# A low-rank adapter and a mixture of experts on one core: logits turned by transposes, h turned inside down for the last tiles, smaller first loads

## The reference

```python
# x [4, 512, 512]; adapter of a batch row a = itok[b]
base = einsum('bsi,oi->bso', x, W_base)
h    = einsum('bsi,ji->bsj', x, Wt)
z    = einsum('bsj,brj->bsr', h, A[a])            # rank 16
l    = einsum('bsr,bor->bso', z, B_w[a])
y    = base + einsum('bso,po->bsp', l, Wp) * scaling[a]
logits = y @ gate_w.T                             # 16 experts
w, e = top_k(softmax(logits), 2);  w = w / sum(w)
g, u = y @ w_gate[e].T, y @ w_up[e].T             # 512 -> 352
out  = x + sum_k w_k * (silu(g) * u) @ w_down[e].T
```

## Time and profile before

| | |
|---|---|
| median of 3 runs | 377.56 us (377.18 to 378.63) |
| the profiled execution | 377.08 us, its span 375.1 us |
| busy share of the span | PE 95%, PEld 84%, DVE 52%, ACT 48%, POOL 34% |
| the chain that ended last | PE 82%, DVE 8%, DMA 4% |
| moved by DMA | 74.26 MB, mean 198 GB/s |

### The profile page before, as it was taken

One profiled execution on the slowest core, in us unless ns is written; L12 is line 12 of the kernel. 1 busy time (PEld: TensorE's weight loads), 2 busy tenths in 40 slices (PEclk: granted clock), 3 DMA queues, 4 the chain that ended last, 5 costly groups with the idle time before them and its releaser, 6 DMA issues.

```text
span 375.1 us, 7604 instructions
## 1 busy us (share of the span) xinstructions
PE 356.9 (95%) x2069; PEld 316.7 (84%) x2069; DVE 195.1 (52%) x269; ACT 178.3 (48%) x242; POOL 128.9 (34%) x85
## 2 busy tenths in 40 slices
PE   8999999998899999999999999999999999999970
PEld 4677787787789999999999999999999999999940
DVE  0485599793264627272654826548262655654210
ACT  1487621521455463645547455474555456644120
POOL 0000000023513524554454645546355455132311
PEclk9999999999899999999999999999999999999986
DMA  7994753736877675949487794857948476822230
GB/s 249 407 476 149 288 197 108 276 109 232 294 259 222 169 249 89 314 92 315 85 244 215 225 310 82 260 187 215 311 93 262 110 223 189 260 32 30 32 55 7
DMA packets 29632, 74.26 MB, mean 198 GB/s; under 512 B 3776, under 2 KB 3904, under 8 KB 29504
## 3 DMA queue, kind: packets, MB, share of 16 engines
q1 hardware_dynamic: 20624, 54.79, 41.7%
q0 software_dynamic: 8960, 18.89, 23.2%
HBM read 61.08 MB, written 19.92 MB: 216 GB/s over the span
## 4 chain that ended last, share of the span: by engine, by line
PE 82%; DVE 8%; DMA 4%; issue 2%; SPq 2%; ACT 1%; POOL 0%; ACTq 0%; DVEq 0%; POOLq 0%
PE bank L626 40%; PE bank L643 22%; PE bank L559 5%; PE bank L604 3%; PE bank L397 2%; PE bank L498 2%; PE bank L500 2%; PE bank L499 2%; DMA wb_sb<-wb 2%; SPq L342 2%; DMA xg<-y_rows,gidx 1%; DVE oh_m L1001 1%; PE bank L425 1%; PE bank L480 1%; DMA y_rows<-y_st 1%
## 5 line engine op out<-in xcount | busy, mean ns | idle before, releaser
L1111 POOL DMA_INDIRECT out<-ys,sidx x40 | 70.2, 1756 | 141.2 <-ACT ys L772 72.7
L1094 POOL DMA_INDIRECT xg<-y_rows,gidx x40 | 58.2, 1455 | 97.9 <-issue 88.0
L336 DVE TENSOR_TENSOR w_lo<-w_raw,w_hi (+2 forms) x32 | 76.1, 2379 | 21.4 <-ACT w_hi L334 19.2
L626 PE MATMUL bank<-w_hi,xt_hi 128*128 x320 | 80.5, 333 | 0.0
L626 PE MATMUL bank<-w_hi,xt_lo 128*128 x320 | 77.2, 322 | 0.0
L626 PE MATMUL bank<-w_lo,xt_hi 128*128 x320 | 77.1, 322 | 0.0
L334 ACT ACTIVATE w_hi<-w_raw (+2 forms) x32 | 64.8, 2024 | 6.3 <-issue 4.5
L763 ACT ACTIVATE sg<-bank 128x352 f32<-128x352 f32 x40 | 18.6, 465 | 80.7 <-PE bank L626 79.8
L626 PEld LDWEIGHTS bank<-w_hi,xt_lo 128*128 128x128 f32 x320 | 55.8, 188 | 0.0
L626 PEld LDWEIGHTS bank<-w_lo,xt_hi 128*128 128x128 f32 x320 | 55.7, 188 | 0.0
L626 PEld LDWEIGHTS bank<-w_hi,xt_hi 128*128 128x128 f32 x320 | 54.1, 189 | 0.1
(11 more groups left out here) (168 smaller groups left out, 376.7 us busy)
## 6 DMA issues: line engine op xcount, KB each, us to landing
w_raw<-wall SPq DMA_DIRECT2D x16, 1408.0 KB
w_raw<-wall SPq DMA_DIRECT2D x16, 768.0 KB
x_st<-xt SPq DMA_DIRECT2D x8, 512.0 KB, 12.9
y_rows<-y_st SPq DMA_DIRECT2D x16, 256.0 KB, 2.3
wt_sb<-wt SPq DMA_DIRECT2D x2, 512.0 KB, 5.5
wpt_sb<-wpt SPq DMA_DIRECT2D x2, 512.0 KB, 7.7
wb_sb<-wb SPq DMA_DIRECT2D x2, 512.0 KB, 7.2
wbt_sb<-wbt SPq DMA_DIRECT2D x2, 512.0 KB, 8.6
```

The costliest lines, as they stand in the source:

```text
L336: e.tensor_tensor(w_lo[:, bass.ds(dst, n)], raw, hi, ALU.subtract).then_inc(own, 1)
L626: mm = e.matmul(bank[2 + 2 * s + t % 2][:, 0:INTER], a, w[:, bass.ds(at + (k * GU + s * INTER), INTER)], start=k == 0 and a is hi and w is ...
L1094: e.indirect_dma_start(out=xg[t % NXG][:], out_offset=None, in_=y_dram, in_offset=bass.IndirectOffsetOnAxis(ap=gidx[:, t:t + 1], axis=0)). ...
L1111: e.indirect_dma_start(out=out, out_offset=bass.IndirectOffsetOnAxis(ap=sidx[:, t:t + 1], axis=0), in_=ys[t % NYS][:], in_offset=None, bou ...
```

## The change

1. **First loads.** A and B come as 64 columns each; B is repeated to 128 columns by a copy on VectorE (`bw_s`). The gate rows and the scaling lie in `cst`; a copy on VectorE spreads the gate rows (`gt_s`), and `gate_rows` writes 64 columns a part. `wt` is loaded and used in four pieces, `cst` comes ahead of `wb`, `adp` behind it.
2. **Logits.** `logits_turn` transposes the 32 rows of a chunk; VectorE sums the halves of all chunks in one reduction.
3. **Places** in TensorE's program are pairs of chunk and k: ranks two k later, table products and need_turn later, x_turn(0) inside chunk 15. On VectorE the last steps of `oh_q` come ahead of w_lo's halves for tile 0.
4. **Tiles from 32 on.** h_turn(t) stands inside down(t-1), ahead of its last k; ACT and VectorE write `ht` of tile t in iteration t, and VectorE splits gu ahead of `y_low`.
5. **The end.** SP, not POOL, waits for the last scatters.

```diff
-C_TURN, C_RANKS, C_WORDS, C_LOAD, C_SPLIT, C_TABLES, C_NEED = 3, 5, 7, 7, 10, 11, 12
+C_WORDS, C_LOAD, C_SPLIT = 7, 7, 10
+AT_TURN, AT_RANKS, AT_TABLES, AT_NEED, AT_X = (3, 1), (5, 2), (12, 1), (12, 3), (CH - 1, 2)
...
@@ SP: loads
-            for s in range(3):
-                load(small_sb[:, s], small[:, s], d_small[s])
-                big, src, done = ((wt_sb, wt, d_wt), (wpt_sb, wpt, d_wpt), (wb_sb, wb, d_wb))[s]
-                for i, half in enumerate(halves):
-                    load(big[:, half], src[:, half], done[i])
-                if s == 1:
-                    load(scl_sb[:], scl, d_scl)
-                    load(adp_sb[:], adp, d_adp)
-                    load(cs[:], cst, d_cst)
+            load(at_s[:], at, d_small[0])
+            for k in range(KH):
+                load(wt_sb[:, k], wt[:, k], d_wt[k])
+            load(bw_in[:], bw, d_small[1])
+            for i, half in enumerate(halves):
+                load(wpt_sb[:, half], wpt[:, half], d_wpt[i])
+            load(cs[:], cst, d_cst)
+            load(wb_sb[:, halves[0]], wb[:, halves[0]], d_wb[0])
+            load(wb_sb[:, halves[1]], wb[:, halves[1]], d_wb[1])
+            load(adp_sb[:], adp, d_adp)
...
@@ SP: end
+            count = tile_count(e)
+            lasts = [e.snap(((count + (NYS - 1 - i)) // NYS) * 16) for i in range(NYS)]
+            for i in range(NYS):
+                e.wait_ge(d_s[i], lasts[i])
+            e.sem_inc(p_turn, 1)
...
@@ TensorE: logits_turn
-                    mm = e.matmul(bank[5][:, c * NEXP:(c + 1) * NEXP], lt_sb[b % 2][:, r * P:(r + 1) * P],
-                                  cs[0:G2, C_RNK:C_RNK + NEXP], start=True, stop=True)
+                    mm = e.transpose(bank[5][:, c * G2:(c + 1) * G2], lt_sb[b % 2][:, r * P:(r + 1) * P], ident[0:G2, 0:G2])
...
@@ TensorE: chunks 3 to 15
-                y_base(c, range(1))
-                if c == C_TURN:
-                    logits_turn(3)
-                if c == C_RANKS:
-                    ranks()
-                y_base(c, range(1, 2))
-                if c == C_TABLES:
-                    e.wait_ge(v_ohm, 1)
-                    slot_tables(bank[4], 0, 2)
-                if c == C_NEED:
-                    need_turn()
-                y_base(c, range(2, KH))
+                for k in range(KH):
+                    if (c, k) == AT_TURN:
+                        logits_turn(3)
+                    if (c, k) == AT_RANKS:
+                        ranks()
+                    if (c, k) == AT_TABLES:
+                        e.wait_ge(v_ohm, 1)
+                        slot_tables(bank[4], 0, 2)
+                    if (c, k) == AT_NEED:
+                        need_turn()
+                    if (c, k) == AT_X:
+                        count = tile_count(e)
+                        words = {0: tile_word(e, 0)}
+                        x_turn(e, count, 0)
+                    y_base(c, range(k, k + 1))
                 y_rank(c)
...
-                if c == CH - 2:
-                    count = tile_count(e)
-                    words = {0: tile_word(e, 0)}
-                    x_turn(e, count, 0)
...
@@ TensorE: down, and the tiles
                     for k in range(KI):
+                        if t + 1 >= NFULL and t + 1 < NTILE and k == KI - 1:
+                            h_turn(t + 1)
...
-                    if t >= 3:
+                    if 3 <= t <= NFULL:
                         h_turn(t - 1)
...
@@ ACT: the tiles
-                    if t >= 3:
+                    if 3 <= t <= NFULL:
                         h_evac(t - 1)
...
                     if t < NTILE:
                         silu(t)
+                    if NFULL <= t < NTILE:
+                        h_evac(t)
                     if t + 1 < NTILE:
                         split_weights(e, count, t + 1, word, "dn", a_dn)
...
@@ VectorE: start
+            e.wait_ge(d_small[1], 16)
+            e.tensor_copy(bw_s[:].rearrange("p k (i r) -> p k i r", i=P // RR),
+                          bw_in[:].unsqueeze(2).to_broadcast([P, KH, P // RR, RR])).then_inc(v_bw, 1)
             e.wait_ge(d_cst, 16)
+            gt_in = cs[:, C_GT:C_GT + KH * NEXP].rearrange("p (k n) -> p k n", n=NEXP)
+            e.tensor_copy(gt_s[:], gt_in.unsqueeze(2).to_broadcast([P, KH, NBATCH, NEXP])).then_inc(v_gt, 1)
             e.wait_ge(d_adp, 16)
...
@@ VectorE: routing
-            lg = bank[5][:, 0:CH * NEXP].rearrange("p (c n) -> p c n", n=NEXP)
+            lg = sh2[:]
+            step(e.tensor_reduce(lg, bank[5][:].rearrange("p (c h n) -> p c n h", h=2, n=NEXP), AX_X, ALU.add))
...
@@ VectorE: the tiles
-                    if t >= 3:
+                    if 3 <= t <= NFULL:
                         h_low(t - 1)
-                    if t == 1:
+                    if t == 1 or NFULL <= t < NTILE - 1:
                         split_weights(e, count, t + 1, word, "gu", v_gu)
...
-                    if 2 <= t < NTILE - 1:
+                    if 2 <= t < NFULL:
                         split_weights(e, count, t + 1, word, "gu", v_gu)
                     if t < NTILE:
                         product(t)
+                    if NFULL <= t < NTILE:
+                        h_low(t)
                     if t + 1 < NTILE:
                         split_weights(e, count, t + 1, word, "dn", v_dn)
...
@@ POOL: end
-            lasts = [e.snap(((count + (NYS - 1 - i)) // NYS) * 16) for i in range(NYS)]
-            for i in range(NYS):
-                e.wait_ge(d_s[i], lasts[i])
-            e.sem_inc(p_turn, 1)
```

More of the change, by code:

```diff
@@ L79, with build @@
 SKIP = 4096
-C_ID, C_IQ, C_TOK, C_ADP, C_AT, C_BEF, C_TOP, C_RNK, C_SEL, CW = (
-    0, P, P + TQ, *(P + TQ + CH + i for i in range(5)), P + TQ + CH + 4 + RANK, 2 * P + TQ + CH + 4 + RANK)
+C_ID, C_IQ, C_TOK, C_ADP, C_AT, C_BEF, C_TOP, C_RNK, C_SEL, C_SCL, C_GT, CW = (
+    0, P, P + TQ, *(P + TQ + CH + i for i in range(5)), *(P + TQ + CH + 4 + RANK + i for i in (0, P, P + 1, P + 1 + KH * NEXP)))
 R_TRI, R_ONE, R_REV, R_THR, R_CUM, R_TH3, R_IM, RW = 0, P, 2 * P, 2 * P + 16, 2 * P + 32, 2 * P + 288, 2 * P + 293, 3 * P + 293
-def build(nc, cst, rcst, small, adp, scl, wt, wpt, wb, wbt, xt, x, wall, out):
+def build(nc, cst, rcst, at, bw, adp, wt, wpt, wb, wbt, xt, x, wall, out):
     with ExitStack() as ctx:
@@ L128, in build @@
         r_lo0 = region(o_lo, SLOT)
-        small_sb = r_lo0("small_sb", [P, 3, KH, P], F32)
+        at_s, bw_in = [r_lo0(n, [P, KH, RR], F32) for n in ("at_s", "bw_in")]
+        bw_s = r_lo0("bw_s", [P, KH, P], F32)
+        gt_s = r_lo0("gt_s", [P, KH, NBATCH, NEXP], F32)
         wb_sb = r_lo0("wb_sb", [P, KH, H], F32)
@@ L174, in build @@
         adp_sb = r_b("adp_sb", [P, NBATCH], I32)
-        scl_sb = r_b("scl_sb", [P, 1], F32)
         r_y = region(o_b, KH * H * 4)
@@ L219, in build @@
         y_dram = nc.dram_tensor("y_rows", [NTOK, H], F32, kind="Internal").ap()
-        d_cst, d_rc, d_adp, d_scl = [sem("d_" + n) for n in ("cst", "rc", "adp", "scl")]
-        d_small = [sem("d_" + n) for n in ("at", "bw", "gt")]
-        d_wt, d_wpt, d_wb, d_wbt = [[sem(f"d_{n}{i}") for i in range(2)] for n in ("wt", "wpt", "wb", "wbt")]
+        d_cst, d_rc, d_adp = [sem("d_" + n) for n in ("cst", "rc", "adp")]
+        v_bw, v_gt = sem("v_bw"), sem("v_gt")
+        d_small = [sem("d_" + n) for n in ("at", "bw")]
+        d_wt = [sem(f"d_wt{i}") for i in range(KH)]
+        d_wpt, d_wb, d_wbt = [[sem(f"d_{n}{i}") for i in range(2)] for n in ("wpt", "wb", "wbt")]
         d_x = [[sem(f"d_x{b}_{i}") for i in range(2)] for b in range(NBATCH)]
@@ L398, in k_sum, with low_rank @@
                 return mm
[L400 to L405, removed]
+            def low_rank(dst, a, big, landed):
+                for k in range(KH):
+                    if k * len(landed) % KH == 0:
+                        e.wait_ge(landed[k * len(landed) // KH], 16)
+                    mm = k_sum(dst, [(a[:, k], big[:, k])], first=k == 0, last=k == KH - 1)
                 return mm
@@ L1178 @@
     gt = chunks(get["L0_ffn_gate_w"].T)
[L1179 to L1180 removed]
     adp = np.repeat(get["itok_B_0_3"][None, :], P, axis=0)
[L1182 removed]
+    cst[:, C_SCL] = np.tile(np.repeat(get["L0_cond_scaling"], RANK), P // RR)
+    cst[:, C_GT:C_GT + KH * NEXP] = gt.reshape(P, -1)
     gu = np.concatenate([get[n].transpose(0, 2, 1).reshape(NEXP, KH, P, INTER) for n in ("L0_ffn_w_gate", "L0_ffn_w_up")], axis=3)
@@ L1188 @@
     arrays = {
-        "cst": cst, "rcst": rcst, "small": small, "adp": adp, "scl": scl,
+        "cst": cst, "rcst": rcst, "at": at, "bw": bw, "adp": adp,
         "wt": chunks(get["L0_cond_Wt"]), "wpt": chunks(get["L0_cond_Wp"].T),
```

40 lines of the change are left out of this document (18 added, 22 removed).

## The result

In 20 runs each, in turn on one chip, the changed kernel took 376.56 us (374.02 to 378.77) and the kernel before 378.71 (374.76 to 381.47): ratio 0.9943, interval 0.9915 to 0.997, 2.15 us or 0.57% faster. The forecast was 6.7 us. The profiled execution took 377.5 us with a span of 375.7. That is 0.4 us more than the profiled execution of before; e5 shows what chance added to it.

The account below looks back on a forecast made before the run. TensorE, busy 95% of the span, was taken to bound the kernel. Terms -4.0 + 2.1 - 1.0 - 1.8 - 2.0 = -6.7 gave 370.4 against 377.08, or 370.9 us beside the 377.56 median; range 368.0 to 375.0.

Parts of the forecast that it names:

- Start, -1.0: First loads up to the first y product: smaller loads let VectorE give x_lo about 1.0 us earlier.
- wb is 1.2 to 1.4 us earlier: Load stream at the start: 0.49 MB less ahead of wb at 340 GB/s brings it 1.2 to 1.4 us earlier.
- 1.0 earlier, not 1.2: VectorE at the start: adp loaded behind wb delays the masks, so x_lo comes 1.0 us earlier rather than 1.2.
- Turn, -2.7: Logits' turn on TensorE: 16 transposes take 1.0 us where 32 records took 3.7, saving 2.7 us.
- its rival of transposes that don't overlap: Logits' turn: 16 records without overlap cost what 32 overlapping did, 2.7 us more, 373.6 us; chance 0.02.
- Ranks no gain, tables -0.3: Later places on TensorE: ranks wait as long as before, table products no longer wait for oh_m, saving 0.3 us.
- Tiles 32 on, +2.1: Tiles from 32 on: h_turn inside down waits for hh in tiles 32, 33 and 35, costing 2.1 us together.
- The 0.95 in tiles 33 and 35: Tiles 33 and 35: silu behind ACT's dn and gu splits makes hh late, so h_turn waits 0.95 us in each.
- in all other tiles hh comes 0.1 before its turn: Tiles from 32 on except 32, 33 and 35: hh is ready 0.1 us ahead of h_turn, so no wait.
- Tail: Last tile to the end: down(39) starts 1.0 us earlier and its nine products run at full clock, saving 1.8 us.
- DRAIN, -2.0: Kernel end: with SP waiting, POOL's DRAIN starts behind the last scatter, still takes 4.23 us, and saves 2.0 us.
- the rival that gave it nothing: Kernel end: the DRAIN itself waits for the last transfers, so the tail gives only -2.8, 372.9 us; chance 0.20.

Follow-up runs that it names:

- e5: The changed kernel, unchanged, profiled in one more execution: 374.55 us.
- e9: The changed kernel, unchanged, timed again on another chip beside the kernel before: 373.72 us, ratio 0.9911.
- e10: Changed kernel with h turned inside down for the last tile only, plus 12 more warm-up products between the first loads: 371.37 us, ratio 0.9844 to the kernel before.
- e11: Changed kernel with h turned inside down for the last tile only, and adp loaded ahead of cst: 370.06 us, ratio 0.9833 to the kernel before.
- e4: Kernel before with only the waits for the last scatters moved from POOL to SP: 375.07 us, ratio 0.9951.

## Why the prediction was wrong

The measured -2.15 us lie outside the range: off the 377.56 of before they give 375.4, and the range ended at 375.0. The -3.4 of e9 would give 374.2, just inside it, and are half of the forecast's -6.7. The direction was right. By its own steps:

- **Start, -1.0: failed, measured -0.1.** (The turn starts at 35.94 on average in the nine profiles of this start without a fall, e10 and e11 left out, and at 36.08 in the five of the old one.) Two steps failed. The first is "wb is 1.2 to 1.4 us earlier", bytes divided by 340 GB/s: the gate rows, which wait for wb, start 0.5 earlier (13.28 on average in the twelve profiles without e10, against 13.80). The second is "1.0 earlier, not 1.2", which counted back from w_base_lo as if adp's delay had room. adp lands at some 14.8 us and VectorE then works without a pause until x_lo: in each of the nine profiles the first y product starts 6.64 or 6.65 us behind the start of mask, the step that reads adp. With adp ahead, e11 gets 0.5 back, about what the stream gave. On top, in 2 of 13 profiled executions of the new start the clock fell, at 18.8 and 18.3, for about 2.4 us at the turn's start (38.55 and 38.20 against 35.94). None of the five profiles with the old start has that fall, but 2 of 13 against 0 of 5 doesn't show that it belongs to the new start.
- **Turn, -2.7: right.** Measured -2.5 at the turn, 16 transposes in 1.3 us, the reduction 0.69 for 0.7. The Trainium skill (TensorE: Matmul & The Clock Gate, PE-mode transpose) has about 275 ns for a transpose of 128x128 bf16; paid in full for each of the 16 smaller float32 ones it would have made this part slower. The rows show 0.22 for one, but 16 in 1.3, so the prediction was right to set it aside, and its rival of transposes that don't overlap is refuted.
- **Ranks no gain, tables -0.3:** right together with the turn: 2.7 from both between the turn's start and the last y row, against 3.0 forecast. Without the new places the turn would have kept 1.8. The hand-over takes nothing back: from the last y row to tile 3 it is 26.6 us before and 26.7 in e9, both with the clock's fall there.
- **Tiles 32 on, +2.1: too small.** The 0.95 in tiles 33 and 35 came as 0.94 and 0.97, with the cause named. The failed step is "in all other tiles hh comes 0.1 before its turn": VectorE's w_lo and xt_lo were followed in tile 32 alone, at 0.2. They are ahead of hh in 34 and 36 too, and cost 0.5 to 0.6 in each of the three. Measured +2.9.
- **Tail: down(39) 0.9 nearer (forecast -1.0) and at full clock (-1.55, forecast -1.8): right.** In all 12 profiles with an idle of 0.9 to 1.02 the nine products took 2.4 us or less; with 1.87 to 1.93 they took 3.2 to 3.9 in five of six, and why e4's took 2.35 stays open.
- **DRAIN, -2.0: half.** The step that failed is the 4.23 us behind an early start of the DRAIN: it began early, as forecast, but a DRAIN that begins early lasts until the rows have landed. But it ends 3.2 behind that instead of 4.2, in all 13 profiles of that kind, so the rival that gave it nothing was not right either: -1.0.

Measured terms: -0.1 - 2.7 + 2.9 - 0.9 - 1.55 - 1.0 = -3.35. e9's -3.4 is as near as that partly by chance, since its interval runs from -4.4 to -2.3. The forecast's other 3.35 went at the DRAIN (1.0), the start (0.9), the tiles from 32 on (0.8), the tail before the DRAIN (0.35) and turn, ranks and tables (0.3). What lacks on the chip of the first result, 1.2, stays open: half of the changed kernel's runs there had a lower mean clock and were slower, but the kernel before was slower there too (378.71 against 376.7 to 377.1 on the others), and no profile tells the two apart.

One of the losses was avoidable. The earlier h_turn pays only in the last tile, where it takes 0.9 us of idle and the clock's fall away; in the seven others it exposes hh. With it there alone the kernel is 6.2 to 7.2 us faster than before.

## What to carry to other kernels

Before a step is moved forward in a steady loop, its producers have to be followed for a whole period of the schedule, on every engine between them, not for the iteration where the first wait is seen. Work that shortens a serial tail belongs in the last iteration alone. And a gain that is left when one engine's chain is shortened has to be checked against the other engine's: the turn lost 0.7 us of 2.5 at the ranks until these were moved too.
